# Attention scores of two heads in the two halves of the array, with three score tasks a pair

## The chip, the cores and the metric

The kernel runs on one core of one Trainium2 chip. A core has TensorE (PE), VectorE (DVE), ScalarE (ACT), GpSimd (POOL), and SyncE (SP), which here only issues DMAs. Each engine works through its own list of instructions in order, and they meet at semaphores. The metric is the device time of one execution in microseconds; the kernel before takes 745.94 us (median of 3 runs, 744.32 to 747.05).

## The reference

Two blocks on an input of 2 batches x 512 positions x 512 channels. Block 0 is attention with 32 heads of 16 channels, times a gated feed-forward, plus the input; block 1 (a small recurrent net and an octonion feed-forward) is not touched by the change beyond the names of its PSUM banks. What matters is block 0's attention:

```python
qkv = hidden_states @ qkv_w + qkv_b
q, k, v = jnp.split(qkv, 3, axis=-1)            # 32 heads of 16
q = _rope(q, cos, sin)
k = _rope(k, cos, sin)
scores = jnp.einsum('bqhd,bkhd->bhqk', q, k) * scale
scores = scores + (1.0 - causal) * MASK_VAL
probs = jax.nn.softmax(scores, axis=-1)
ctx = jnp.einsum('bhqk,bkhd->bqhd', probs, v).reshape(b, s, e)
return ctx @ out_w + out_b
```

## The kernel before

Every fp32 product is made of three products of a reduced type (`f32r`): high x high, high x low, low x high. For a projection these are three matmuls over 128 rows, here called a triple (`passes`, lines 913 to 916). For the scores the parts are stacked on the contraction rows: a head's 16 channels give 48 rows. The weights of block 0 come as units of 128x512; SP loads a unit (`raw`), ACT or POOL writes its high part, POOL its low part (`split`), PE uses it.

**Scores.** Heads are worked through in 16 pairs a batch, four heads (two pairs) being a group. `q_st` holds a group's queries, both heads of a pair one above the other on 96 rows. `kz` holds the keys with zeros: for either head there is a copy in which the other head's 48 rows are zero, so that a matmul over 96 rows gives one head's scores. Each pair has two kinds of task. Five tasks of `score` (lines 932 to 945) put queries on PSUM's partitions; DVE takes the row maxima of them (`row_maxima`, a reduce or an operation that adds the causal mask and keeps the maximum), joins them, and PE turns them (`max_turn`) so that ACT can write them as extra rows into `q_st`. Five tasks of `score_T` (947 to 954), 8 slots later, compute the transposed scores over 100 rows, with the maximum subtracted by the four extra rows; `kz` has the values -1 on these rows, set on DVE at the start (line 1537) after POOL has cleared `kz` (721). ACT takes the exponential (1294), POOL clears the part above the diagonal (752), and PE multiplies with V (1065), four heads side by side in four strips of 32 columns of the array.

**Order.** Each batch is a list of slots (`SLOTS`), and each engine's program walks it. A slot s has score task s, score_T task s - 8, perhaps a piece of probs x V, and the triples of the next projection and feed-forward units (`triples_in`), which fill PE's time. Units 0 and 1 (Q and K of the first quarter) and 2 to 5 (V) come before the slots. The rotary result of Q and K is written to DRAM by head (`write_rows`) and read back stacked (`read_rows`), which takes up to the first score. Three PSUM banks (`score_ps`) are shared by both kinds of task in turn; two banks (`turn_ps`) take all transposes. After the slots with scores come 11 slots of the feed-forward's down projection, then the output projection.

## Time and profile before

| | |
|---|---|
| runs | 744.32, 745.94, 747.05 us |
| profiled execution | 744.25 us, its span 742.1 us |
| PE, DVE busy | 653.9 us (88%), 453.2 us (61%) |
| POOL, ACT busy | 403.7 us (54%), 280.3 us (38%) |
| mean granted clock of TensorE | 0.964 |
| triples of all projections (lines 914 to 916), 240 each | 100.9, 96.7 and 96.0 us |
| scores (938, 952) and transposed maxima (928) | 29.3, 65.4 and 20.0 us |

Times are in microseconds from the span's start. Matmuls are pipelined, so one that is listed with 0.39 us may be followed by the next 0.23 us later: for PE the distance from start to start tells what one costs. The fraction after an operation in a timeline, in brackets, is the idle time of the engine just before it and who ended it. The granted clock is a share of full speed.

### The profile page before, as it was taken

How to read it: one execution, taken by the hardware profiler on the slowest of the kernel's cores; microseconds unless marked ns; L12 is line 12 of the kernel's file. 1: busy time of each engine (PE TensorE's matmuls, PEld its weight loads, DVE VectorE, ACT ScalarE, POOL GpSimd, SP SyncE). 2: the span in 40 equal slices, each digit the busy share in tenths (PEclk: the TensorE clock that was granted, in tenths of full speed). 3: DMA queues.
4: the chain of work that ended last, by engine and by line, in shares of the span. 5: the costliest groups of instructions: out<-in, count | busy, mean ns of one | idle time of the engine just before them, and what ended most of it. 6: DMA issues, size and time to landing. Idle time of an engine off the chain costs nothing. (4 is left out here: it accounts for less than half of the span.)

```text
span 742.1 us, 9827 instructions
## 1 busy us (share of the span) xinstructions
PE 653.9 (88%) x3229; PEld 468.4 (63%) x3229; DVE 453.2 (61%) x1086; ACT 280.3 (38%) x501; POOL 403.7 (54%) x593
## 2 busy tenths in 40 slices
PE   1967899999989998889999998989798979797993
PEld 1756566667756776666666765678676655555571
DVE  4977778756534493887785562459454434756347
ACT  2413445444543411344444455351222534142441
POOL 6476455545343556646554534439725778344465
PEclk9989999999999999999999999999998989999997
DMA  8287575753222226967575316534200000000003
GB/s 263 80 288 227 129 203 134 212 134 77 75 72 72 57 71 198 310 151 200 140 198 144 85 36 228 190 101 160 76 1 0 1 0 1 1 0 1 0 1 113
DMA packets 59731, 82.21 MB, mean 111 GB/s; under 512 B 18057, under 2 KB 26505, under 8 KB 59681
## 3 DMA queue, kind: packets, MB, share of 16 engines
q1 hardware_dynamic: 56016, 70.31, 33.4%
q10 hardware_dynamic: 3664, 11.28, 4.1%
q8 instruction: 26, 0.43, 0.2%
q14 instruction: 25, 0.20, 0.1%
HBM read 63.75 MB, written 26.47 MB: 122 GB/s over the span
## 5 line engine op out<-in xcount | busy, mean ns | idle before, releaser
L731 POOL TENSOR_TENSOR w_lo<-raw,w_hi 128x512 fp32r<-128x512 f32 x98 | 129.3, 1321 | 81.7 <-ACT w_hi L1251 76.8
L1294 ACT ACTIVATE probs_T<-score_ps 128x512 f32<-128x512 f32 x160 | 95.8, 599 | 156.2 <-PE score_ps L952 132.9
L1444 DVE CUSTOM_DVE_ANT_0 score_ps<-score_ps,causal 128x128 f32<-128x128 f32 (+2 forms) x256 | 103.0, 447 | 52.9 <-PE score_ps L938 28.6
L914 PE MATMUL proj_ps<-xn_hi,w_hi 128*128 128x512 f32 x240 | 100.9, 420 | 12.2 <-DVE by_sin L1520 7.5
L752 POOL TENSOR_SCALAR_AFFINE_SELECT probs_T<-probs_T 128x256 f32<-128x256 f32 (+1 forms) x160 | 56.5, 362 | 96.6 <-ACT probs_T L1294 96.6
L915 PE MATMUL proj_ps<-xn_hi,w_lo 128*128 128x512 f32 x240 | 96.7, 403 | 0.0
L916 PE MATMUL proj_ps<-xn_lo,w_hi 128*128 128x512 f32 x240 | 96.0, 400 | 0.0
L952 PE MATMUL score_ps<-q_st,kz 100*128 100x512 f32 (+3 forms) x256 | 65.4, 316 | 8.6 <-DVE row_max L1444 8.4
L952 PEld LDWEIGHTS score_ps<-q_st,kz 100*128 100x128 f32 x256 | 47.8, 188 | 26.0 <-DVE row_max L1444 15.1
L914 PEld LDWEIGHTS proj_ps<-xn_hi,w_hi 128*128 128x128 f32 x240 | 47.1, 196 | 22.7 <-issue 12.3
L916 PEld LDWEIGHTS proj_ps<-xn_lo,w_hi 128*128 128x128 f32 x240 | 46.7, 194 | 11.4
L729 POOL TENSOR_SCALAR w_hi<-raw 128x512 fp32r<-128x512 f32 x56 | 36.4, 650 | 31.2 <-PE proj_ps L916 24.3
L915 PEld LDWEIGHTS proj_ps<-xn_hi,w_lo 128*128 128x128 f32 x240 | 47.3, 197 | 8.6
L1065 PE MATMUL ctx_ps<-probs_T,V 128*32 128x128 f32 (+3 forms) x512 | 47.7, 445 | 0.0
L869 POOL TENSOR_TENSOR hsL<-hidden_T,hsH 128x256 fp32r<-128x256 f32 x44 | 34.8, 805 | 21.9 <-ACT hsH L1378 21.9
L1498 DVE SCALAR_TENSOR_TENSOR gate_silu<-gate_tanh,proj_ps 128x512 f32<-128x512 f32 x22 | 15.1, 686 | 36.9 <-ACT gate_tanh L1260 24.4
L1592 DVE TENSOR_TENSOR hsl<-hidden_T,hsh 128x512 fp32r<-128x512 f32 x22 | 16.9, 769 | 32.4 <-ACT hsh L1309 32.4
L1444 DVE DVE_READ_ACCUMULATOR2_ANT row_max<- 128x1 f32 x256 | 35.8, 140 | 0.0
L740 POOL TENSOR_TENSOR rows_lo<-turned_rows,rows_hi 128x512 fp32r<-128x512 f32 x16 | 20.7, 1295 | 25.8 <-ACT rows_hi L1229 25.8
L938 PE MATMUL score_ps<-kz,q_st 96*128 96x512 f32 x64 | 29.3, 457 | 5.8 <-DMA kz<-rows 5.8
L1251 ACT ACTIVATE w_hi<-raw 128x512 fp32r<-128x512 f32 x42 | 26.2, 624 | 17.8 <-PE turn_ps L916 6.3
L1438 DVE TENSOR_REDUCE row_max<-score_ps 128x2 f32<-128x512 f32 x32 | 22.0, 688 | 16.3 <-PE score_ps L940 15.9
(288 smaller groups left out, 1496.0 us busy)
## 6 DMA issues: line engine op xcount, KB each, us to landing
raw<-w SPq DMA_DIRECT2D x98, 256.0 KB, 2.7
rows<-rows_hi SPq DMA_DIRECT2D x32, 256.0 KB, 3.6
arranged<-tern SPq DMA_DIRECT2D x96, 85.0 KB
q_st<-rows SPq DMA_DIRECT2D x16, 384.0 KB, 4.5
kz<-rows SPq DMA_DIRECT2D x32, 192.0 KB, 4.9
...
```

The lines of the kernel that those rows point to most:

```text
L729: nc.gpsimd.tensor_scalar(w_hi[n % SPLIT][:, :], raw[n % RAW][:, :], 1.0, 0.0, ALU.mult, ALU.add).then_inc(hi_done, 1)
L731: nc.gpsimd.tensor_tensor(w_lo[n % SPLIT][:, :], raw[n % RAW][:, :], F32(w_hi[n % SPLIT][:, :]), ALU.subtract).then_inc(unit_ready, 1)
L752: nc.gpsimd.affine_select(out=blocks, in_=blocks, pattern=[[0, n], [1, P]], compare_op=ALU.is_ge, fill=0.0, base=0, channel_multiplier=-1) ...
L869: nc.gpsimd.tensor_tensor(hsL[d % HS][:, :], hidden1_T[:, f, 256 * pr:256 * pr + 256], F32(hsH[d % HS][:, :]), sub).then_inc(hs1_ready, 1)
L914: nc.tensor.matmul(acc, lh, rh, start=first, stop=False)
L915: nc.tensor.matmul(acc, ll, rh, start=False, stop=False)
L916: return nc.tensor.matmul(acc, lh, rl, start=False, stop=last)
L938: return nc.tensor.matmul(acc[:, :], q[:, 3 * P:], k[:, i, :], start=True, stop=True)
L952: m = nc.tensor.matmul(acc[:, c:c + S - kt * P], k[:, hh, kt * P:(kt + 1) * P], q[:, kt * P:], start=x == 0, stop=True, skip_group_check=x ...
L1065: m = nc.tensor.matmul(ctx_ps[32 * h:32 * h + 32, kt * P:S], V[:, kt, (4 * g + h) * 32:(4 * g + h + 1) * 32], probs_T[(gp + h // 2) % 3][: ...
L1294: nc.scalar.activation(probs_T[gp % 3][:, 512 * i:512 * i + 512], score_bank(b, ("b", s - LAG))[:, :], ACT.Exp, scale=0.25).then_inc(probs ...
L1444: m = nc.vector.tensor_tensor_reduce(out=block, in0=block, in1=causal[:, S - w:], scale=1.0, scalar=-3e38, op0=ALU.add, op1=ALU.max, accum ...
```

## The change

Each head of a pair gets contraction rows of its own: head 0 has rows 0 to 49 and head 1 rows 64 to 113, in `q_st` as in the new `k_st` that takes the place of `kz`. The first two of the 50 rows belong to the maximum (in `k_st` the value -1, written to DRAM once by SP from a constant `edges` and read back with the rows), the other 48 are the head's stacked parts. A score task is now one matmul (or two) for each head, into two PSUM banks; a pair has three tasks of each kind instead of five, `LAG` goes from 8 to 5, and a batch has 53 slots with scores instead of 88. Row tasks compute no more than the part up to the diagonal block. There are two banks for the rows and two for the transposed scores, no sharing, and one bank (`one_turn_ps`) for transposes during the scores. POOL's clearing of `kz` and DVE's six operations on it are gone, as are one reduce and one joining step a pair; ACT copies the turned maxima in two pieces. The second Q and K units move from 6 and 7 to 8 and 9, and eight triples (units 6 and 7) instead of four precede slot 0. `rope_first` now has all three operations that read the projection. The high part of a hidden tile for the down projection is made two slots ahead rather than one, and the `arranged` copies are spread over slots 9 to 51.

```diff
-B_BANKS = [[(0, 0, 0)], [(0, 1, 0), (0, 3, 384)], [(0, 2, 0), (1, 2, 256)], [(1, 0, 0)], [(1, 1, 0), (1, 3, 384)]]
-LAG = 8
-SCORE_SLOTS = 5 * PAIRS + LAG
+A_TILES = [[(3, 0)], [(2, 0), (0, 384)], [(1, 0)]]
+B_TILES = [[(0, 0)], [(1, 0), (3, 384)], [(2, 0)]]
+WIDTH = (512, 512, 256)
+TASKS = 3 * PAIRS
+LAG = 5
+SCORE_SLOTS = TASKS + LAG
...
-Q_UNIT, K_UNIT, V_UNIT = (0, 6, 12, 18), (1, 7, 13, 19), 2
+Q_UNIT, K_UNIT, V_UNIT = (0, 8, 12, 18), (1, 9, 13, 19), 2
...
-    return max(-1, (k - KC) * SCORE_SLOTS // (TRIPLES - KC))
+    return max(-1, (k - 2 * KC) * SCORE_SLOTS // (TRIPLES - 2 * KC))
...
-    return next((g for g in range(1, GROUPS) if (1 if g == 1 else max(10 * g - 10, unit_slot(K_UNIT[g // 2]) + 9)) == s), None)
+    return next((g for g in range(1, GROUPS) if (1 if g == 1 else max(6 * g - 6, unit_slot(K_UNIT[g // 2]) + 7)) == s), None)
...
-            for n in range(3):
-                nc.gpsimd.memset(F32(kz[n][:, :, :, :]), 0.0).then_inc(zeroed, 1)
...
+            def stacks(b, j, hh):
+
+                n = (GROUPS * b + j // 2) % 3
+                rows = slice(64 * hh, 64 * hh + HEAD_ROWS)
+                return q_st[n][rows, j % 2, :], k_st[n][rows, j % 2, :]
+
+            def scores(b, j, x):
+
+                for part, (qt, c) in enumerate(A_TILES[x]):
+                    for hh in range(2):
+                        q, k = stacks(b, j, hh)
+                        m = nc.tensor.matmul(score_ps[:, hh, c:c + (qt + 1) * P], q[:, qt * P:(qt + 1) * P], k[:, 0:(qt + 1) * P],
+                                             start=part == 0, stop=True, skip_group_check=part > 0)
+                m.then_inc(score_done, 1)
...
                 for s in range(SLOTS):
                     if score_in(s):
...
-                        if bank_free(b, ("a", s)):
-                            pe.wait_ge(*bank_free(b, ("a", s)))
-                        score(score_bank(b, ("a", s)), b, j, i).then_inc(score_done, 1)
+                        if s:
+                            pe.wait_ge(part_ready, TASKS * b + s)
+                        scores(b, j, x)
+                    if prob_in(s):
+                        j, x = prob_in(s)
+                        if x == 0:
+                            pe.wait_ge(*copied(b, ("max", j)))
+                        if s > LAG:
+                            pe.wait_ge(probs_ready, TASKS * b + s - LAG)
+                        scores_T(b, j, x)
...
+                for qt, c in A_TILES[x]:
+                    w = (qt + 1) * P
+                    for hh in range(2):
+                        block = score_ps[:, hh, c:c + w]
+                        m = nc.vector.tensor_tensor_reduce(out=block, in0=block, in1=causal[:, S - w:], scale=1.0, scalar=-3e38, op0=ALU.add,
+                                                           op1=ALU.max, accum_out=row_max[:, j % 2, 2 * qt + hh:2 * qt + hh + 1])
...
-            for n in range(3):
-                for hh in range(2):
-                    rows = kz[n][2 * ROWS:2 * ROWS + 4, :, hh, :]
-                    nc.vector.tensor_scalar(rows, F32(rows), extreme[2 * ROWS:2 * ROWS + 4, hh:hh + 1], None, ALU.add).then_inc(extreme_set, 1)
```

PE's list around the first piece of the first probs x V product of the first batch, before. `score_ps<-kz` is a task with queries on the partitions, `score_ps<-q_st` a transposed one, `ctx_ps` the product with V, `turn_ps` the turning of the maxima.

```order
L938 MATMUL score_ps<-kz_75,q_st_88 128x512
L914 MATMUL proj_ps<-xn_hi,w_hi_103 128x512
L915 MATMUL proj_ps<-xn_hi,w_lo_108 128x512
L916 MATMUL proj_ps<-xn_lo,w_hi_103 128x512
L952 MATMUL score_ps<-q_st_87,kz_74 128x256 x2
L1065 MATMUL ctx_ps<-probs_T_91,V 32x512 x2
L1065 MATMUL ctx_ps<-probs_T_92,V 32x512 x2
L938 MATMUL score_ps<-kz_75,q_st_88 128x512
L914 MATMUL proj_ps<-xn_hi,w_hi_103 128x512
L915 MATMUL proj_ps<-xn_hi,w_lo_108 128x512
L916 MATMUL proj_ps<-xn_lo,w_hi_103 128x512
L952 MATMUL score_ps<-q_st_87,kz_74 128x512
```

The same place in PE's list now (`score_ps<-k_st` with queries on the partitions, `scoreT_ps` transposed, `one_turn_ps` the maxima):

```order
L943 MATMUL one_turn_ps<-ident,max_cols 34x128 x4
L1081 MATMUL ctx_ps<-probs_T_91,V 32x512 x2
L1081 MATMUL ctx_ps<-probs_T_92,V 32x512 x2
L957 MATMUL score_ps<-k_st_74,q_st_88 128x384 x2
L957 MATMUL score_ps<-k_st_74,q_st_88 128x128 x2
L966 MATMUL scoreT_ps<-q_st_87,k_st_73 128x256 x2
L929 MATMUL proj_ps<-xn_hi,w_hi_105 128x512
L930 MATMUL proj_ps<-xn_hi,w_lo_110 128x512
L931 MATMUL proj_ps<-xn_lo,w_hi_105 128x512
L929 MATMUL proj_ps<-xn_hi,w_hi_105 128x512
L930 MATMUL proj_ps<-xn_hi,w_lo_110 128x512
L931 MATMUL proj_ps<-xn_lo,w_hi_105 128x512
```

Both kinds of task now stand together in a slot, each as pairs of matmuls for the two heads, and two triples follow where there were one or two.

SP's list around the load of the third group's rows, before (`raw` a weight unit, `rows<-` the rotary rows to DRAM, `q_st`, `kz` the rows back):

```order
L632 DMA raw_97<-w 128x512 [waits unit_ready]
L640 DMA rows<-rows_hi_83 16x8x512 [waits rows_hi_ready]
L640 DMA rows<-rows_hi_83 16x8x512
L642 DMA rows<-rows_lo_85 16x8x512 [waits rows_lo_ready]
L632 DMA raw_98<-w 128x512 [waits unit_ready]
L656 DMA q_st_88<-rows 96x2x512 [waits extreme_set,rows_stored]
L659 DMA kz_75<-rows 48x2x512 x2
```

And now:

```order
L652 DMA rows<-rows_hi_83 16x8x512 [waits rows_hi_ready]
L652 DMA rows<-rows_hi_83 16x8x512
L654 DMA rows<-rows_lo_85 16x8x512 [waits rows_lo_ready]
L644 DMA raw_97<-w 128x512 [waits unit_ready]
L707 DMA arranged<-tern 64x2x170 [waits tern_stored]
L707 DMA arranged<-tern 64x2x170
L644 DMA raw_98<-w 128x512 [waits unit_ready]
L667 DMA q_st_88<-rows 50x2x512 [waits rows_stored]
L667 DMA q_st_88<-rows 50x2x512
L667 DMA k_st_74<-rows 50x2x512 x2
```

The load stands one weight unit and two copies further behind the rows' writing, and is four DMAs instead of three; it is used from slot 12 on, where it was from slot 20 on.

## Rows read from the trace of the kernel before

**Rows 1.** Busy time by stretch (us, share by engine, PEclk, DMA, GB/s).
```profile
47.30:67.80 20.50, 16.93 (x64) 13.42 (x65) 16.63 (x48) 3.53 (x6) 14.40 (x16) 0.84 0.77 256
67.80:214.50 146.70, 138.38 (x802) 95.90 (x800) 97.72 (x333) 69.37 (x121) 73.59 (x126) 1.00 0.51 135
...
291.60:311.10 19.50, 16.90 (x64) 13.22 (x65) 16.54 (x48) 3.53 (x6) 14.38 (x16) 0.82 0.83 268
311.10:458.50 147.40, 139.02 (x805) 96.46 (x804) 97.56 (x333) 69.18 (x120) 74.27 (x126) 1.00 0.54 144
```

**Rows 2.** Timeline of PE from 612 and 624 us: start, us, engine, line.
```profile
614.41 0.39 PE L1127 MATMUL proj_ps<-down_w,hsL 128*128 128x512 f32 x1
614.73 1.13 PE L1190 MATMUL score_ps<-wk,w1T 64*128 64x512 f32 x4
615.79 0.50 PE L1126 MATMUL proj_ps<-down_w,hsH 128*128 128x512 f32 x1
...
625.28 1.02 PE L1158 MATMUL score_ps<-wk,centre_m 128*128 128x512 f32 x2
...
626.37 0.40 PE L1113 MATMUL ctx_ps<-xm_lo,up_w 128*128 128x512 f32 x1
```

**Rows 3.** Timeline of PE around one probs x V product.
```profile
84.87 0.40 PE L952 MATMUL score_ps<-q_st,kz 100*128 100x256 f32 x2
85.19 1.07 PE L1065 MATMUL ctx_ps<-probs_T,V 128*32 128x512 f32 x8
86.19 0.50 PE L938 MATMUL score_ps<-kz,q_st 96*128 96x512 f32 x1
86.53 0.40 PE L914 MATMUL proj_ps<-xn_hi,w_hi 128*128 128x512 f32 x1
86.77 0.40 PE L915 MATMUL proj_ps<-xn_hi,w_lo 128*128 128x512 f32 x1
```

**Rows 4.** Timeline of all engines, 4 to 10 us.
```profile
4.27 5.29 POOL L721 MEMSET kz<- 128x2048 f32 x3
...
7.95 0.36 DVE L1475 BATCH_NORM_AGGREGATE mean_var<-stat 128x2 f32<-128x6 f32 x4
```

**Rows 5.** Timeline of DVE, 20 to 36 us.
```profile
20.80 8.23 DVE L1537 TENSOR_SCALAR kz<-kz,extreme 4x1024 fp32r<-4x1024 f32 x6
29.06 0.75 DVE L1511 SCALAR_TENSOR_TENSOR by_cos<-proj_ps,qk_bias,rope_cos 128x512 f32<-128x512 f32 x1
...
34.56 0.69 DVE L1527 TENSOR_TENSOR turned_rows<-by_cos,by_sin 128x512 f32<-128x512 f32 x1
```

**Rows 6.** Timeline of PE: the first start, the down stage, the second start.
```profile
24.98 0.17 PE L997 MATMUL turn_ps<-abs_sums,V 128*128 128x3 f32 x1
...
40.24 0.79 PE L914 MATMUL proj_ps<-xn_hi,w_hi 128*128 128x512 f32 x1 [3.97 <-POOL w_lo L731]
...
47.31 0.77 PE L938 MATMUL score_ps<-kz,q_st 96*128 96x512 f32 x1 [2.44 <-DMA kz<-rows]
...
59.85 0.47 PE L914 MATMUL proj_ps<-xn_hi,w_hi 128*128 128x512 f32 x1 [3.57 <-DVE by_sin L1520]
...
214.56 0.50 PE L914 MATMUL score_ps<-w_hi,hsh 128*128 128x512 f32 x1 [1.93 <-DVE hsl L1592]
...
291.66 0.47 PE L938 MATMUL score_ps<-kz,q_st 96*128 96x512 f32 x1 [3.41 <-DMA kz<-rows]
```

**Rows 7.** Groups of lines by shape (count, busy, mean ns, idle before).
```profile
L731 POOL TENSOR_TENSOR w_lo<-raw,w_hi 128x512 fp32r<-128x512 f32 x98 | 129.3, 1321 | 81.7 <-ACT w_hi L1251 76.8
...
L1444 DVE CUSTOM_DVE_ANT_0 score_ps<-score_ps,causal 128x512 f32<-128x512 f32 x64 | 44.0, 697 | 28.8 <-PE score_ps L938 28.6
...
L729 POOL TENSOR_SCALAR w_hi<-raw 128x512 fp32r<-128x512 f32 x56 | 36.4, 650 | 31.2 <-PE proj_ps L916 24.3 <-DMA raw<-w 6.3
...
L1444 DVE CUSTOM_DVE_ANT_0 score_ps<-score_ps,causal 128x128 f32<-128x128 f32 x128 | 33.3, 322 | 17.9 <-PE score_ps L943 17.6
```

**Rows 8.** The page's DMA issues (count, KB each, median us to landing).
```profile
kz<-rows SPq DMA_DIRECT2D x32, 192.0 KB, 4.9
```

444 lines of the change are left out of this document (212 added, 232 removed).

## The prediction

> **What bounds the kernel now.** I read the table of stretches first, then TensorE's timeline, then who waits for whom. The part that changes is the attention of either batch: its start, and the score stage. In the steady score stage [rows 1] (second and fourth row) PE is busy for 138.38 of 146.70 us at full clock, DVE for 97.72, POOL 73.59, ACT 69.37. So PE sets the pace there, and what it saves in that stage is worth its full price as long as DVE, the next one, does not take over. The two first stretches [rows 1] (first and third row) are different: 20.5 and 19.5 us with a granted clock of 0.84 and 0.82, and DVE busy for 16.63 and 16.54 of them, so there PE waits. TensorE's own timeline shows the places [rows 6]: 3.97 us for a weight split of POOL at 40.24, 2.44 us for the rows that come back from DRAM at 47.31, 3.57 us for DVE's rotary work at 59.85, 3.41 us for the rows again at 291.66.
>
> The profiled execution took 744.25 us (span 742.1), the median of the runs is 745.94. I make the sum against 744.25 and add 1.7 at the end.
>
> **1. Set-up of the first batch: 6.7 us earlier.** POOL's three memsets of kz, 5.29 us, end at 9.56, while DVE has the means ready at 8.31 [rows 4]; without them the norm starts 1.25 us earlier, and all of PE's first work with it. The six small DVE operations on kz, 8.23 us, go too, and they stand ahead of the rotary work of Q and K (29.06 to 35.25) [rows 5]. K's projection ends at about 25.1 [rows 6], with the shift at 23.9, and Q's about 2.7 us before it, so Q's rotation runs 21.2 to 24.2 and K's to 27.3. From K's last addition to the first score matmul before are 47.31 - 35.25 = 12.1 us (ACT's high part, POOL's low part, write, read back); four loads in place of three add about 0.4 (one issue), which gives 39.8. PE's side is later: V's projection ended at 36.27 (40.24 less the 3.97 idle), now 35.0, and then come eight fill triples in place of four, 8 x 0.70 = 5.6 us, so 40.6. POOL must have split units 6 and 7 by then: it starts about 29.3, at some 2.6 us a unit while DVE's ternary work slows it, done at 34.5. First score at 40.6 in place of 47.3, with four triples more behind it.
>
> **2. Set-up of the second batch: 0.3 us later.** There DVE's combining of the batch before bounds the rows; they land where they did, with one issue more. The 3.41 us of waiting [rows 6] is filled with the four extra triples (2.8 us); that work is taken from the score stage, where I count it.
>
> **3. First slots.** Before, ten slots (two pairs) took 20.5 and 19.5 us. Now two pairs are six slots. One maximum over 512 columns costs 0.63 us from start to start, over 128 columns 0.25 (the means 697 and 322 overlap the next start) [rows 7]; a pair's eight are 3.6 us, joining them 0.8 (an estimate: two small operations and their waits), and two rotary units of 3.1 (29.06 to 35.25 for two [rows 5]) fall into these slots. With single score banks (both of the pair in one task), PE asks for the next task only after DVE has read the last: a slot takes at least 0.55 (matmul and its way to DVE) + 1.3 to 1.5. Slot by slot that gives 16.1 us: 4.4 and 3.4 less.
>
> **4. The rest of the score stage: 11.1 us less per batch**, from 146.7 and 147.4, in three parts.
> Two heads in two halves: a matmul of 512 columns takes 0.24 us from start to start [rows 3]. A pair has 2 x 2560 columns, ten times 0.235, or 2.35 us; side by side 1.17. That halves overlap is seen in block 1 [rows 2]: four 64-row passes of 512 columns take 1.06 us (614.73 to 615.79), while two full passes of the same type take 0.85 (625.28 to 626.37, less one matmul of 0.24). One after another the four would be 1.7.
> Against it stands what a change of the array's layout costs. Around a product of probs and V [rows 3] the matmul ahead takes 0.32 in place of 0.24, the product 1.00 in place of 0.86, the one behind it 0.34: 0.32 us for in and out. Around the 64-row passes it is 0.08 ahead and 0.21 inside [rows 2]. I take 0.33. By the order of instructions, each of three slots a pair goes into the new layout and out again: 1.0 us. In four of six slots the neighbour is a probs x V product that changed the layout anyway, which gives back about 0.1 each, 0.3 a pair with the bubbles that the two small matmuls of the old fourth task had. Net 2.35 - 1.17 - 1.0 + 0.3 = 0.48 us a pair, times 14.7 pairs: 7.0 us. The Trainium skill, "TensorEngine Tiling (Array Packing)", section Key Properties, says that a change of the tiling mode drains TensorE, while two tiles of one mode run in parallel. By that rule each of these slots pays, and the trace agrees with its 0.32 us; were the layout change free, the term would be 32 x 1.0 us larger, so 32 us more of gain.
> Triples moved ahead of the stage: three fewer here (one fewer in the first slots), 2.1 us.
> Waits: PE is idle for 8.3 of the 146.7 us [rows 1], 1.9 of them at the stage's end, so some 6.5 are waits, most of them for DVE's maxima. Now DVE's load falls (no separate reduce, no joining of two parts) but a rotary unit's 2.25 us in one piece can delay the next task, about 0.4 each for four units. I take 4.5: 2 us less. Not less than 0 and up to 15 us a batch are its bounds, since DVE works for 97.72 us of 146.7 now, and for some 92 of about 136 then.
>
> **5. A new wait, 5.4 us per batch more.** The rows of the third group are asked for in slot 10 and needed in slot 12; before, slot 11 for slot 20. In SP's order the read stands behind the load of raw unit 21, which waits for POOL's split of unit 17, which waits for the end of unit 12 in slot 9. From then: 0.65 + 1.32 us for the split [rows 7], 0.4 for the load, 1.7 for four issues, 4.9 to landing [rows 8]: 8.9 us, against two slots of 2.35 to 2.45, so 4.0 us of waiting. Behind the waiting matmul stand all of slot 12's tasks. After waits of such a size the clock was at half for some 3 us ([rows 1], first and third row, 0.84 and 0.82), which costs 1.4 us more. Bounds: 0 (the loads run ahead) to 8 (they land late behind the small-packet copies).
>
> **6. Ends.** The high part of the first hidden tile is now made two slots ahead, so the 1.93 us wait of the down stage [rows 6] keeps only the last probabilities and the last unit, about 1 us: 0.9 less, twice. In the second batch ACT waits in slot 53 for copies whose last is issued in slot 51, where it had 25 slots: 1 us, 0 to 4. Exps of 1024 columns, two small copies of the maxima in place of one, masks: ACT and POOL have half their time free, nothing. All else keeps its order.
>
> **Sum.** -6.7 + 0.3 - 4.4 - 3.4 - 2 x 11.1 + 2 x 5.4 - 1.8 + 1 = -26.4: 744.25 becomes 717.9, and with 1.7 for the median 719.5. I write 719.
>
> **Rivals.**
> Rows in time and cheap changes: SP and POOL run ahead, the third group's rows land before slot 12 (-10.8), and a layout change hides half its price behind the next weight load (-16 x 0.5 = -8). For it: the pass count inside one layout change is small and two of the three pieces are below 0.1 us. Against it: the chain of waits in item 5 has no slack. 719 - 19 = 700. Chance 0.20.
> DVE becomes the pace: one pair of score banks means that each of 48 tasks a batch is handed over with PE waiting, where three banks shared the load before. If each hand-over costs 0.25 us, 96 x 0.25 = 24 us: 743, no change. For it: the first stretches [rows 1], where DVE at 81 to 85% held PE up. Against: DVE has a third of its time free in the steady stage. It decides when DVE's slot, 0.55 + maxima + unit, passes PE's 2.85 us. Chance 0.12.
> The halves do not run side by side with this operand type: then each pair loses the 1.17 us and still pays for the layouts, 32 x 1.17 = 37.5: 756.5, slower. It decides if four 64-row fp32 passes [rows 2] say nothing on the reduced type; the trace has no row-split matmul of that type. Also this is how it comes out if the change does not do what it says. Chance 0.06.
> The forecast has the remaining 0.62, with 706 to 731 as its own range.
>
> **How the numbers follow.** What a measurement of this kernel can tell from no change is about 0.5%, 3.7 us: 742 to 750 is the same. Faster: 0.62 + 0.20 + half of 0.12, 0.88. Same 0.05. Slower 0.07, the last rival and a little of the one before. The range reaches from the first rival at 702 to 738, short of the second and third.
>
> **What would show it.** The first score task at 40 to 42 us and the two heads' matmuls starting within 0.1 us of each other; matmuls of neighbours at 0.32 to 0.34 beside a layout change; a wait of 3 to 5 us of PE for k_st or q_st once in either batch, about 30 us behind the first score; the score stage some 7 to 12 us shorter behind its first two pairs; DVE busy for under 75% of it. It is wrong if the pair's matmuls start 0.2 us apart, or if PE's waits for the maxima pass 10 us a batch.

## The result and the profile after

The changed kernel takes 736.07 us (median of 4 runs, 733.23 to 738.93), the kernel before, run beside it, 745.13. The ratio is 0.9875, with an interval of 0.9842 to 0.9908. Measured once more later (label e12 below) it was 0.9828 (0.9797 to 0.9859). So the change gains 9 to 13 us, by the ratios, where 26 were forecast; single edits are compared below with the middle of the two ratios, 0.985. Since these two ratios of one and the same kernel lie 3.5 us apart and each run's own interval reaches 2 to 3 us to either side, a difference by the ratios under 3 us says nothing by itself, and the traces have to decide. One run of e9 took 795 us at a granted clock of 0.75; it is left out of that ratio, and the median given there (713.83 us) would be 713.71 without it. The profiled execution took 734.26 us, its span is 732.5 against 742.1.

The table of stretches of the profile after, cut at the same events as [rows 1] (first score, two pairs later, first product of the down stage):

```profile
40.20:60.00 19.80, 15.57 (x59) 9.86 (x58) 15.52 (x46) 3.31 (x5) 12.53 (x13) 0.83 0.89 306
60.00:200.90 140.90, 131.69 (x827) 81.14 (x827) 93.72 (x305) 73.71 (x106) 73.16 (x112) 0.98 0.51 145
280.60:300.40 19.80, 15.00 (x58) 9.59 (x58) 14.99 (x44) 2.72 (x4) 13.17 (x14) 0.83 0.68 217
300.40:442.70 142.30, 132.16 (x826) 81.35 (x826) 94.53 (x307) 73.58 (x106) 72.33 (x111) 0.97 0.54 155
```

The first two pairs take as long as they did, again at a clock of 0.83. The rest of the score stage is 5.8 and 4.4 us shorter, with a busy PE of 132 us in place of 138, and 9 to 10 us of waiting in place of 8. TensorE's timeline has the places (start, us, what; in brackets the idle time ahead and who ended it):

```profile
40.21 0.50 PE L957 MATMUL score_ps<-k_st,q_st 50*128 50x512 f32 x2
42.84 0.77 PE L929 MATMUL proj_ps<-xn_hi,w_hi 128*128 128x512 f32 x1 [2.13 <-POOL w_lo L744]
...
54.35 0.50 PE L957 MATMUL score_ps<-k_st,q_st 50*128 50x384 f32 x4 [1.96 <-DVE row_max L1459]
...
79.72 0.80 PE L957 MATMUL score_ps<-k_st,q_st 50*128 50x512 f32 x2 [5.31 <-DMA k_st<-rows]
...
200.93 0.47 PE L929 MATMUL score_ps<-w_hi,hsh 128*128 128x512 f32 x1 [1.50 <-DVE hidden_T L1516]
...
220.20 0.65 PE L925 MATMUL one_turn_ps<-ident,ctx_sums 128*128 128x128 f32 x4 [1.78 <-ACT ctx_sums L1338]
...
280.59 0.49 PE L957 MATMUL score_ps<-k_st,q_st 50*128 50x512 f32 x2 [3.25 <-DMA k_st<-rows]
283.21 0.76 PE L929 MATMUL proj_ps<-xn_hi,w_hi 128*128 128x512 f32 x1 [2.13 <-DVE gate_silu L1512]
...
321.10 0.80 PE L957 MATMUL score_ps<-k_st,q_st 50*128 50x512 f32 x2 [5.08 <-DMA k_st<-rows]
...
442.75 0.77 PE L929 MATMUL score_ps<-w_hi,hsh 128*128 128x512 f32 x1 [1.50 <-DVE hidden_T L1516]
```

They answer to [rows 6]: the first score stands at 40.21, where 40.6 was forecast, and without a wait. The wait at slot 12 is there, 5.31 and 5.08 us (the waits for `k_st`). Three kinds of wait are not in the forecast: 2.13 us right behind the first score of either batch, 1.78 us for the sums in the down stage, and 3.25 us for the rows ahead of the second batch, though four triples now fill that gap. Where a row of 512 columns is listed with 0.77 or 0.80 us instead of 0.5 or less, the clock is at half: behind 442.75 the next ones follow at 0.43 us from start to start, behind the wait at 200.93 at 0.23.

Laid end to end on the two profiled spans (the second batch's set-up is counted from the third group of the output projection, 258.36 before and 244.68 after, its down stage to the last norm's first turn, 524.41 and 513.28):

| stretch | before | after | difference | forecast |
|---|---|---|---|---|
| up to the first score | 47.31 | 40.21 | -7.1 | -6.7 |
| batch 0: first two pairs | 20.5 | 19.8 | -0.7 | -4.4 |
| batch 0: rest of the score stage | 146.8 | 140.9 | -5.8 | -6.6 |
| batch 0: down stage | 43.8 | 43.75 | 0 | 0 |
| set-up of batch 1 | 33.3 | 35.9 | +2.6 | +0.3 |
| batch 1: first two pairs | 19.4 | 19.85 | +0.4 | -3.4 |
| batch 1: rest of the score stage | 146.8 | 142.3 | -4.4 | -6.6 |
| batch 1: down stage, output | 66.55 | 70.5 | +4.0 | +1.0 |
| from the last norm to the end | 217.7 | 219.2 | +1.5 | 0 |
| sum | | | -9.6 | -26.4 |

Inside the steady stage the slots are as forecast. One slot's tasks, and the starts of the slots six earlier and six later:

```profile
134.07 0.50 PE L957 MATMUL score_ps<-k_st,q_st 50*128 50x512 f32 x2
...
151.25 0.50 PE L957 MATMUL score_ps<-k_st,q_st 50*128 50x512 f32 x2
151.58 0.40 PE L966 MATMUL scoreT_ps<-q_st,k_st 50*128 50x384 f32 x4
151.91 0.50 PE L929 MATMUL proj_ps<-xn_hi,w_hi 128*128 128x512 f32 x1
152.25 0.40 PE L930 MATMUL proj_ps<-xn_hi,w_lo 128*128 128x512 f32 x1
...
168.42 0.50 PE L957 MATMUL score_ps<-k_st,q_st 50*128 50x512 f32 x2
```

Two matmuls of 512 columns for the two heads take 0.33 us, the four of the next task 0.33, the first full one behind them 0.34: against the 0.235 each of the prediction that is 0.3 us for the way into the layout and out. Two pairs take 17.17 us.

### The profile page after: what moved, and what is told of

Same layout as the page of the kernel before. It is cut to its first block and busy times, and to the rows that moved or that the text cites. A ratio compares the mean times of both kernels' runs of the same rounds, so it can differ in the third digit from the quotient of the medians.

```text
span 732.5 us, 9833 instructions
## 1 busy us (share of the span) xinstructions
PE 644.0 (88%) x3293; PEld 437.5 (60%) x3293; DVE 434.5 (59%) x1016; ACT 288.4 (39%) x469; POOL 392.1 (54%) x559
## 5 line engine op out<-in xcount | busy, mean ns | idle before, releaser
L1459 DVE CUSTOM_DVE_ANT_0 score_ps<-score_ps,causal 128x512 f32<-128x512 f32 (+3 forms) x256 | 120.0, 517 | 91.7 <-PE score_ps L957 91.5
L1312 ACT ACTIVATE probs_T<-scoreT_ps 128x1024 f32<-128x1024 f32 (+1 forms) x96 | 84.7, 883 | 82.8 <-PE scoreT_ps L966 81.8
L930 PE MATMUL proj_ps<-xn_hi,w_lo 128*128 128x512 f32 x224 | 90.2, 402 | 0.0
L957 PE MATMUL score_ps<-k_st,q_st 50*128 50x512 f32 (+3 forms) x256 | 45.6, 393 | 22.3 <-DMA k_st<-rows 13.6
L957 PEld LDWEIGHTS score_ps<-k_st,q_st 50*128 50x128 f32 x256 | 22.1, 188 | 66.2 <-issue 34.9
L764 POOL TENSOR_SCALAR_AFFINE_SELECT probs_T<-probs_T 128x256 f32<-128x256 f32 x128 | 50.2, 414 | 20.1 <-ACT probs_T L1312 19.9
L1237 ACT ACTIVATE q_st<-one_turn_ps 2x512 fp32r<-2x512 f32 x64 | 37.5, 585 | 26.9 <-PE one_turn_ps L943 26.4
L930 PEld LDWEIGHTS proj_ps<-xn_hi,w_lo 128*128 128x128 f32 x224 | 43.8, 196 | 5.4
L1601 DVE TENSOR_TENSOR hsl<-hidden_T,hsh 128x512 fp32r<-128x512 f32 x22 | 16.1, 734 | 43.7 <-ACT hsh L1329 43.7
L1246 ACT ACTIVATE rows_hi<-turned_rows 128x512 fp32r<-128x512 f32 x16 | 10.1, 631 | 75.1 <-DVE turned_rows L1540 75.1
L966 PE MATMUL scoreT_ps<-q_st,k_st 50*128 50x512 f32 (+3 forms) x256 | 37.9, 333 | 0.6 <-ACT probs_T L1312 0.6
L1329 ACT ACTIVATE hsh<-hidden_T 128x512 fp32r<-128x512 f32 x22 | 13.9, 630 | 49.9 <-PE score_ps L931 49.9
```

The costliest lines, as they stand in the source:

```text
L764: m = nc.gpsimd.affine_select(out=halves[:, :, c:c + P], in_=halves[:, :, c:c + P], pattern=[[0, 2], [1, P]], compare_op=ALU.is_ge, fill=0 ...
L930: nc.tensor.matmul(acc, ll, rh, start=False, stop=False)
L957: m = nc.tensor.matmul(score_ps[:, hh, c:c + (qt + 1) * P], q[:, qt * P:(qt + 1) * P], k[:, 0:(qt + 1) * P], start=part == 0, stop=True, s ...
L966: m = nc.tensor.matmul(scoreT_ps[:, hh, c:c + S - kt * P], k[:, kt * P:(kt + 1) * P], q[:, kt * P:], start=part == 0, stop=True, skip_grou ...
L1237: m = nc.scalar.activation(q_st[g % 3][64 * hh:64 * hh + 2, j % 2, :], turn_bank(n)[32 * hh:32 * hh + 2, :], ACT.Copy)
L1312: nc.scalar.activation(probs_T[gp % 4][:, c:c + 2 * w].rearrange("p (h c) -> p h c", h=2), scoreT_ps[:, :, 0:w], ACT.Exp, scale=0.25).then ...
```

## The experiments

Each has one edit on the changed kernel, unless it says otherwise; "less" and "more" are against the changed kernel at 0.985 of the kernel before.

**e1. Gate and hidden product ahead of slot 0's maxima.**

```diff
+                    if s == 0:
+                        for u in units_after(0):
+                            ffn_out(b, u)
                     if score_in(s):
                         row_maxima(b, s)
```

> The changed kernel, with one edit: VectorE works off the gate and hidden product of units 6 and 7 before the row maxima of slot 0 instead of behind them. My theory (the projection banks): TensorE's 2.13 us of waiting in slot 0 of either batch is for the bank that this product frees, not for GpSimd's low part that the profile names in the first batch. Then the wait goes in both batches, with the stretch at half clock behind it: slot 1 starts at about 43.0 instead of 45.67 and at about 283.4 instead of 286.04, and the time falls by 4 to 6 us, to about 731. Rival 1 (GpSimd's low part holds it in the first batch): only the second batch gains, 2 to 3 us, 733.5. Rival 2 (VectorE is the pace of the first two pairs): slot 1 is earlier, slot 6 starts where it did (60.0 and 300.4), time 735 to 736.

Measured: 731.43 us, ratio 0.9806 (0.9767 to 0.9845), 3 us less, which the time alone does not tell from nothing. VectorE's list in the changed kernel shows what it is about (the gate waits behind both maxima):

```profile
40.75 0.70 DVE L1459 CUSTOM_DVE_ANT_0 score_ps<-score_ps,causal 128x512 f32<-128x512 f32 x1 [4.83 <-PE score_ps L957]
...
41.36 0.73 DVE L1459 CUSTOM_DVE_ANT_0 score_ps<-score_ps,causal 128x512 f32<-128x512 f32 x1
...
42.01 0.68 DVE L1512 SCALAR_TENSOR_TENSOR gate_silu<-gate_tanh,proj_ps 128x512 f32<-128x512 f32 x1
```

It ends at 42.69, TensorE goes on at 42.84; the low part that the profile named ends at 42.77 and belongs to unit 9, not to the unit that TensorE was at. With the edit, TensorE in batch 0:

```profile
42.89 0.47 PE L929 MATMUL proj_ps<-xn_hi,w_hi 128*128 128x512 f32 x1 [1.45 <-DVE gate_silu L1512]
```

Slot 1 follows slot 0 by 3.97 and 3.58 us in place of 5.46 and 5.45, and the first two pairs take 17.6 and 18.0 us in place of 19.8 and 19.85. In batch 1 the wait is gone, in batch 0 the gate now waits for ScalarE's tanh, which stands behind its ternary pieces. Rival 1 falls, the bank it is. Rival 2 falls in batch 1, where slot 12 starts 38.2 us behind slot 0 in place of 40.5, though 1.4 and 1.7 us of waiting at slot 4 stay. In batch 0 it has something for it: the same kernel without the edit took 17.9 us for the two pairs in e12, and slot 12 starts at 79.29 for 79.72, since VectorE's maxima hold TensorE in slots 6 to 8 (0.84, 0.54 and 0.82 us) where they hardly did. The profiled execution was the slowest of the six (735.24): both its down stages began at half clock, in the changed kernel's profile only the second.

**e2. The third group's rows asked for two slots earlier.**

```diff
-... max(6 * g - 6, unit_slot(K_UNIT[g // 2]) + 7)) == s), None)
+... max(6 * g - 6, unit_slot(K_UNIT[g // 2]) + 5)) == s), None)
```

> The changed kernel, with the rows of the third group asked for in slot 8 instead of slot 10. My theory: the wait at slot 12 (5.31 and 5.08 us) is the chain of weight load, four issues and landing behind the read, so it falls by what the read is issued earlier. The rows are written at 64.73 and lie in DRAM some 5 us later, so the read goes out at about 69.8 instead of 72.5 and lands at about 76.9, where TensorE stands ready at 74.4: 2.5 us of waiting in place of 5.3, in either batch; with a shorter stretch at half clock the time falls by 5 to 7 us, to about 730. Rival (the landing is set by the traffic of the small arranged copies and weight loads, or GpSimd's splits run dry because SyncE stands at the rows): the wait stays above 4.5 us or turns into a wait for w_lo, and the time is 735 to 737.

Measured: 726.14 us, ratio 0.9749 (0.9709 to 0.979), 8 us less. SyncE's list of the changed kernel has the chain (start, us of issuing):

```profile
62.54 0.33 SPq L644 DMA_DIRECT2D raw<-w  x1
62.92 1.16 SPq L652 DMA_DIRECT2D rows<-rows_hi  x2
64.12 0.61 SPq L654 DMA_DIRECT2D rows<-rows_lo  x1
67.14 0.33 SPq L644 DMA_DIRECT2D raw<-w  x1
67.52 1.40 SPq L707 DMA_DIRECT2D arranged<-tern  x2
72.12 0.33 SPq L644 DMA_DIRECT2D raw<-w  x1
72.50 0.77 SPq L667 DMA_DIRECT2D q_st<-rows  x2
73.31 0.74 SPq L667 DMA_DIRECT2D k_st<-rows  x2
```

The last write took 3.8 us from issue to landing, so the rows lay in DRAM at 67.9, 4 us before 72.12, where GpSimd's split (it ends at 72.10) let the load ahead of them go. With the edit slot 12 waits

```profile
76.84 0.50 PE L957 MATMUL score_ps<-k_st,q_st 50*128 50x512 f32 x2 [0.88 <-DVE row_max L1459]
...
315.66 0.50 PE L957 MATMUL score_ps<-k_st,q_st 50*128 50x512 f32 x2 [2.29 <-DMA k_st<-rows]
```

0.9 and 2.3 us, and no longer at half clock. The theory holds, and in batch 0 the rows are in time (2.5 us of waiting were expected); slots 6 to 12 take 16.5 and 17.9 us instead of 19.7 and 20.7. In batch 1 four loads of X stand ahead of the rows' writing (see e9).

**e3. The sums turned one slot later.** `ctx_in` counts from slot 18 instead of 17.

> The changed kernel, with the turning of each group's sums one slot later (two slots behind the last product with V, as it was before the change, instead of one). My theory: TensorE's waits for ctx_sums at the end of the score stage (0.79, 0.80) and in the down stage (1.78, 1.78) are ScalarE's copy with nothing of TensorE's beside it, so all four go: 5.1 us, to 731. Rival (they are handed on to the waits that follow, hidden_T at the stage's end and xn_lo in the down stage): less than 1.5 us, 735.

Measured: 728.39 us, ratio 0.9769 (0.9742 to 0.9796), 6 us less. Of the four waits the two in the down stages go and the two at the stage's end stay:

```profile
203.07 0.66 PE L925 MATMUL one_turn_ps<-ident,ctx_sums 128*128 128x128 f32 x4 [0.81 <-ACT ctx_sums L1338]
204.20 0.71 PE L929 MATMUL score_ps<-w_hi,hsh 128*128 128x512 f32 x1 [0.47 <-DVE hidden_T L1516]
```

The wait for hidden_T falls from 1.50 to 0.47, since VectorE's work on the turned sums is no longer ahead of it. So half of the theory was right, and the size came out by another split. The profiled execution, the slowest of the six, is only 2.0 us shorter: in the score stages a wait of 1.2 us for the turned rows (`ctx_rows`) comes in each. The second batch's down stage is 65.9 us long in place of 70.5; some 2.6 of that (thirteen matmuls 0.2 us further apart) is a stretch at half clock that followed the longer wait in the changed kernel (row at 442.75).

**e4. The rotary work behind the next slot's maxima.**

```diff
                     for u in units_after(s - 1):
                         if u in QK_OF:
+                            rope_first(b, u)
                             rope_second(b, u)
...
-                        else:
-                            rope_first(b, u)
```

> The changed kernel, with VectorE's three rotary operations of a Q or K unit moved from the end of a slot to behind the next slot's row maxima. My theory: the waits for row_max at slot 4 (1.96 and 1.67 us) and the 0.9 to 0.5 us ones of slots 6 to 8 are these 2.2 us of VectorE ahead of the maxima of a task whose bank TensorE wants, so they fall by two thirds or more: slot 6 starts at about 58.3 and 298.7, and the time falls by 3 to 5 us, to 732. Rival (the projection bank is now freed later and the unit behind waits, or the wait moves one slot on because VectorE is full in these slots anyway): 735 to 737, with waits for by_sin in place of row_max.

Measured: 738.20 us, ratio 0.9919 (0.989 to 0.9948), 5 us more. The first wait for row_max goes, and others come:

```profile
53.25 0.47 PE L929 MATMUL proj_ps<-xn_hi,w_hi 128*128 128x512 f32 x1 [1.32 <-POOL w_lo L744]
...
59.68 0.47 PE L929 MATMUL proj_ps<-xn_hi,w_hi 128*128 128x512 f32 x1 [1.13 <-DVE by_sin L1529]
```

The rival holds: the bank comes free later, and GpSimd's split with it. My theory had the cause of the wait right and the worth of the edit wrong: two pairs of batch 0 take 17.2 us for 17.9 in e12, but slot 9 starts 26.5 us behind slot 0 for 26.4 there, and the rest of the score stage is 145 us long in either batch in place of 141 to 142.

**e5. Both heads on the same rows.**

```diff
-                rows = slice(64 * hh, 64 * hh + HEAD_ROWS)
+                rows = slice(0, HEAD_ROWS)
```

> The changed kernel, but the matmuls of both heads of a pair take their operands from rows 0 to 49, so that they can't use different halves of the array (head 1's scores are head 0's: its own are left out). My theory: the two halves work side by side, and that is worth a pair's ten passes of 512 columns at 0.235 us less half of them, 1.17 us; here they run one after another, so the time rises by 32 x 1.17 = 37 us or a little less where VectorE's maxima are waited for anyway, to 768 to 774, and the two heads' matmuls start 0.2 us apart instead of together. Rival (the halves save little, the gain of the score stage is the shorter row tasks): a rise under 12 us.

Measured: 768.97 us, ratio 1.0318 (1.0281 to 1.0356), 35 us more, or 1.09 us a pair where 1.17 were worked out; in the traces the score stages behind the first two pairs are 33.1 us longer, 1.18 for each of their 28 pairs. A slot's tasks now:

```profile
152.37 0.74 PE L957 MATMUL score_ps<-k_st,q_st 50*128 50x512 f32 x2
152.95 0.68 PE L966 MATMUL scoreT_ps<-q_st,k_st 50*128 50x384 f32 x4
```

0.58 us from the first to the second task, where it was 0.33. The halves do work side by side on the reduced type; without that the kernel is 24 us slower than the one before.

**e6. A triple between the slot's two tasks.** `fill` is called for the first triple between `scores` and `scores_T`, for the others behind it.

> The changed kernel, with the slot's first triple between its score task and its transposed task, where the two tasks stand side by side. That adds one way into the 64-row layout and one out in each of 43 slots a batch. My theory (the price read from TensorE's timeline, 0.3 us for in and out): 86 x 0.3 = 26 us more, less what VectorE's and ScalarE's waits gain from the later use, so 755 to 762. Rival (the layout change hides behind the weight load, 0.1 us): 8 us or less more, up to 745.

Measured: 766.58 us, ratio 1.0295 (1.0266 to 1.0325), 33 us more, where 755 to 762 was expected, and 0.385 us for each of the 86 added ways in and out. The rival is out, and the theory's price of 0.3 is somewhat too small:

```profile
152.30 0.50 PE L957 MATMUL score_ps<-k_st,q_st 50*128 50x512 f32 x2
152.73 0.51 PE L929 MATMUL proj_ps<-xn_hi,w_hi 128*128 128x512 f32 x1
153.07 0.40 PE L930 MATMUL proj_ps<-xn_hi,w_lo 128*128 128x512 f32 x1
```

A task alone behind a product with V takes 0.43 us, and the matmul behind it 0.34: 0.3 us over two ordinary ones. Against the changed kernel's trace the 36 slots from slot 12 on are 13.3 and 12.4 us longer, 0.36 a slot; what slots 6 to 11 lose is partly taken from the wait at slot 12 (3.99 and 3.90 us). And 2.1 of the 31.3 us between the two profiled executions lie behind the last norm, where nothing was changed, so 0.385 has scatter in it. The 0.06 between 0.30 and 0.36 is open.

**e7. The set-up work put back.**

```diff
+            for n in range(3):
+                for stack in (q_st, k_st):
+                    nc.gpsimd.memset(F32(stack[n][:, :, :]), 0.0).then_inc(zeroed, 1)
...
+                for hh in range(2):
+                    part = (q_st, k_st)[hh][n][96:100, :, :]
+                    nc.vector.tensor_scalar(part, F32(part), 1.0, None, ALU.add).then_inc(extreme_set, 1)
```

> The changed kernel, with the set-up work that the change took out put back: GpSimd clears 12 KB a partition (here the stacks of q_st and k_st) ahead of everything, and VectorE does six additions over 4 x 1024 elements ahead of the rotary work. My theory (item 1 of the prediction): the norm starts 1.25 us later and the rotary work waits for 8.2 us of VectorE, so the first score starts at about 47 instead of 40.2 and the time rises by 6.7 us, to 743. Rival (it is covered by the eight triples and V's projection, which have to end before the first score anyway): 2 us or less.

Measured: 743.84 us, ratio 0.9983 (0.996 to 1.0006), 10 us more. (The clearing is six pieces of 1024 elements, 24 KB a partition as in the kernel before, not 12.) The first score starts at 48.54:

```profile
48.54 0.50 PE L962 MATMUL score_ps<-k_st,q_st 50*128 50x512 f32 x2 [1.09 <-DMA k_st<-rows]
```

That is 8.3 us later, not 6.7, with 1.09 us of waiting for the rows, whose reading is slower than in the kernel before (e15). Item 1 stands: without it the change would be worth almost nothing.

**e8. The edits of e1, e2 and e3 together.**

> The changed kernel with the three edits that gained in the runs before: gate and hidden product ahead of slot 0's maxima, the third group's rows asked for in slot 8, the turning of the sums one slot later. If each wait is its own cost they add up. From the marks in the traces: 2.2 + 1.9 us of the first six slots, 3.2 + 2.8 at slot 12, 1.0 and 1.8 twice at the stage's end and in the down stage, and about 2.4 of half clock behind them: 17 us less than the changed kernel, 718 to 720. Rival (VectorE is the pace of the first twelve slots, so the two first edits share one gain): 724 to 727.

Measured: 716.43 us, ratio 0.9605 (0.9582 to 0.9629), 18 us less, about the sum of the three (17 by their ratios; the profiled executions differ by 17.3). The theory holds, though in batch 0 the wait in slot 0 stays at 1.99 us and the two pairs at 19.3: the edit of e1 works here in batch 1 alone, where they take 16.3.

**e9. Two more edits on e8**, `ffn_tanh(b, 6)` behind the second ternary piece, and X reloaded in slot 14.

> The three edits, and two more that touch one batch each. Batch 0: ScalarE takes the tanh of unit 6 between its ternary pieces instead of behind them, since in the run before the gate product waited for it until 42.84 and TensorE still stood 1.99 us in slot 0. Batch 1: SyncE reloads X in slot 14 instead of slot 6, where its four issues (1.76 us) stood ahead of the writing of the third group's rows. My theory: slot 0's wait in batch 0 goes and with it the half clock behind it, so the first six slots take about 16.4 us instead of 19.3; the wait at slot 12 of batch 1 falls from 3.14 to about 1.4 us. Together 4 to 6 us less than the three edits (716.4): 711. Rival (the first pairs of batch 0 are VectorE's anyway): 715.

Measured: 713.83 us, ratio 0.9556 (0.9528 to 0.9583), 3.7 less than e8 by the ratios. The wait in slot 0 of batch 0 is gone, and two pairs take 16.4 us where e8 had 19.3; slots 6 to 12 of batch 1 take 16.6 in place of 18.7. Both steps came as expected, but the first two pairs of batch 1, which neither touches, take 17.5 in place of 16.3, and the sum is short of the 4 to 6 us. 16.4 is what the forecast had given the first two pairs (16.1).

**e10. On e8, the third rotary operation a slot later**, as before the change.

> The three edits, with the third rotary operation given back to the second part, a slot later, as it was before the change. If VectorE's 2.2 us in one piece are what TensorE waits for at slot 4 (1.96 and 1.03 us) and in slots 6 to 8 (0.9, 0.5, 0.8), each of these falls by up to 0.75: 3 to 5 us less in all, 712. Rival (what the run with all three operations behind the maxima showed: the bank is freed a slot later, and a wait for by_sin takes its place): 716 or a little more.

Measured: 722.20 us, ratio 0.9684 (0.9648 to 0.9719), 6 us more than e8. The first waits shrink (0.87 at slot 4), but by_sin is waited for and the rest of the score stage is 2.1 and 2.7 us longer. So the change's one-piece `rope_first`, which the forecast had as a small loss, is a gain: 6 us by the ratios, 3.5 between the profiled executions.

**e11. On e8, the parts of a hidden tile one slot ahead** (`down_in(s + 1)`).

> The three edits, with the high and low part of a hidden tile made one slot ahead instead of two, as before the change. My theory: two slots ahead gained the start of the down stage only if ScalarE is not kept from other work; the wait for xn_lo (1.63 us, before 0.98) is ScalarE's high parts ahead of xn_hi, so it falls to 1.0, but the stage's start waits again, 1.9 us in place of 0.47. Sum +1 us a batch: 718. Rival (the two-slot lead gained nothing): 715 to 716.

Measured: 712.59 us, ratio 0.9555 (0.9529 to 0.9581), 3.7 less than e8. My theory is wrong: the stage's start gets shorter too, one wait of 0.65 us in place of 0.79 and 0.47, and that for xn_lo is 0.98 for 1.63. In both batches that is 2.5 us; the rest of the gain is not located at the edit.

**e12. The changed kernel again.**

> The changed kernel once more, without an edit, beside the same runs of the kernel before as the three others. It says what the comparisons of single edits can tell: if the ratio is again 0.984 to 0.991, read_early's 0.9749 and ctx_late's 0.9769 are gains of 7 to 9 us, more than their marks in the traces (5 to 6); if it is lower, the gains by the marks are right. In its trace the same waits should stand (2.13, 1.7 to 2.0, 5.3, 5.1, 1.5, 1.78), while the stretches at half clock may lie elsewhere. I expect 736 with the waits the same, and the part from the last norm to the end at 218 to 220 us.

Measured: 733.83 us, ratio 0.9828 (0.9797 to 0.9859). The waits are the same (2.13, 1.69, 5.65, 1.49, 1.78, 3.16, 5.07), but the first two pairs of batch 0 take 17.9 us in place of 19.8, since the stretch behind the wait of 2.13 us ran at full clock. The wait of 2.13 us, and the one at slot 12:

```profile
43.08 0.47 PE L929 MATMUL proj_ps<-xn_hi,w_hi 128*128 128x512 f32 x1 [2.13 <-DVE gate_silu L1512]
...
79.58 0.80 PE L957 MATMUL score_ps<-k_st,q_st 50*128 50x512 f32 x2 [5.65 <-DMA k_st<-rows]
```

So 1.9 us of that term is not the kernel's. They are not won either: TensorE then waits for the maxima in slots 6 to 8 (0.90, 0.48 and 0.81 us) and 0.3 us longer at slot 12, which starts at 79.58 for 79.72. My expectation also said what a ratio below 0.984 would mean: that the gains of e2 and e3 are those that their traces show, under 6 us, and not the 8 and 6 us against 0.985. From the last norm to the end it takes 219.2; over all kernels here, none of which touches that part, it is 217.7 to 221.4, so the table's +1.5 is no effect of the change that could be told.

**e13. One slot ahead alone, on the changed kernel.**

> The changed kernel with one edit: the parts of a hidden tile one slot ahead instead of two. If the lead keeps ScalarE and VectorE from the work that TensorE waits for, the waits at the stage's start (0.80 for ctx_sums, 1.50 for hidden_T) shrink together to some 1.5 us, xn_lo from 1.63 to 0.98, and the turn's 1.78 stays, since it is the turning one slot early: the time falls by 3 to 4 us, 731. Rival (the gain seen on top of the other edits needs the later turning): 734 to 736, with a wait of 1.9 us for hsl at the stage's start, as in the kernel before.

Measured: 728.38 us, ratio 0.9774 (0.9751 to 0.9797), 6 us less. The wait of 1.78 us goes as well, which I had put down to the early turning. ScalarE's list of the changed kernel shows why:

```profile
218.51 0.63 ACT L1329 ACTIVATE hsh<-hidden_T 128x512 fp32r<-128x512 f32 x1 [2.16 <-PE score_ps L931]
219.05 0.61 ACT L1268 ACTIVATE w_hi<-raw 128x512 fp32r<-128x512 f32 x1
219.57 0.58 ACT L1338 ACTIVATE ctx_sums<-ctx_ps 128x512 f32<-128x512 f32 x1
```

There are two buffers for the high part. Two slots ahead, ScalarE waits at hsh until TensorE has ended its last product of the slot, and only then comes to the sums that TensorE wants next. One slot ahead, it is through with them when TensorE gets there:

```profile
229.33 0.66 PE L980 MATMUL one_turn_ps<-ident,xn_later 128*128 128x128 f32 x4 [0.98 <-DVE xn_lo L1450]
...
442.49 0.50 PE L929 MATMUL score_ps<-w_hi,hsh 128*128 128x512 f32 x1 [2.27 <-DVE hsl L1601]
```

The wait for xn_lo is 0.98 us again, and at the stage's start one wait of 2.27 us stands in place of 0.80 and 1.50. So the lead gained nothing there, and the later turning (e3) was a second cure for the same illness: the two gave 6 us each alone and 9.7 together (e11). In the traces the lead costs 4.9 us, two waits of 1.78 and twice 0.65 at xn_lo.

**e14. All six edits.**

> All six edits: gate and hidden product first, third group's rows in slot 8, the turning one slot later, tanh of unit 6 earlier, X reloaded in slot 14, hidden parts one slot ahead. The first two to four touch the start and slot 12, the others the down stages, so they should add: 712.6 with the lead of one slot, less 2.6 for the two last edits of the start: 709 to 711. Rival (what is left is VectorE's rotary work in slots 4 to 8 and the gains overlap there): 712 to 713.

Measured: 709.30 us, ratio 0.9513 (0.9493 to 0.9534). On top of e8 they add: its 0.9605 less the 0.0049 of e9 and the 0.0050 of e11 is 0.9506.

**e15. On e14, a stack read by one load over 128 partitions.**

```diff
-                    for hh in range(2):
-                        sp.dma_start(F32(stack[n % 3][64 * hh:64 * hh + HEAD_ROWS, :, :]),
-                                     rows_d[b][t][c][h + hh:h + 4:2].rearrange("p r s -> r p s")).then_inc(stack_in[n % 3], 16)
+                    sp.dma_start(F32(stack[n % 3][:, :, :]),
+                                 rows_d[b][t][c][h:h + 4].rearrange("(p a) r s -> (a r) p s", a=2)).then_inc(stack_in[n % 3], 16)
...
```

> The six edits, and each stack read by one load over 128 partitions (64 rows a head, 14 of them padding that is written to DRAM once) instead of two over 50: two loads of 512 KB in place of four of 200 KB in all 800. My theory (a load over 50 partitions moves at half the rate): from VectorE's last rotary operation of the second batch to the first score it takes 10.5 to 11 us, as in the kernel before, instead of 13.0, so the wait for k_st at the second batch's first score falls from 3.26 to 0.5 to 1 us, those left at slots 6 and 12 go, and the time falls by 2 to 4 us, to about 706, if the padding's writes cost nothing. Rival (the traffic beside it is the cause, and 28% more bytes make it worse): the wait for k_st stays at 3 us or more, 709 to 712.

Measured: 707.49 us, ratio 0.9491 (0.9468 to 0.9515). By the ratios that is 1.6 us under e14, within what the two intervals leave open. The wait for k_st at the second batch's first score falls from 3.26 to 1.39 us, but at slot 12 of the first batch one of 1.60 comes. From the end of VectorE's last rotary operation ahead of the second batch's first score to that score it takes 11.2 us, in e14 and in the changed kernel 13.05, in the kernel before 10.5. The busy share of the 16 DMA engines (tenths) and the traffic in 40 slices, in the changed kernel from 272.5 to 280.6:

```profile
DMA  0000000341366666776746999979999999998899
GB/s 10 0 0 0 0 0 10 111 51 30 142 243 263 233 233 202 243 182 142 172 131 222 344 324 273 293 192 314 222 192 212 172 162 162 162 162 162 243 405 364
```

and in e15 from 261.5 to 267.6:

```profile
DMA  0000000099318999597799999999999999999999
GB/s 0 0 0 0 0 0 0 0 94 107 40 67 322 363 363 403 201 295 228 282 416 403 403 403 430 430 376 403 403 403 430 390 403 416 376 403 430 376 376 416
```

The changed kernel's engines stand at 0.6 to 0.7 in the first half of the read, until the weight loads behind it join in, e15's at 0.9, with 28% more bytes. The form of the loads is the cause, not the traffic beside them.

**e16 and e17. Which property of the form.** e16 is e15 with four loads over 64 partitions; e17 is e14 (50 rows, no padding) with each load split into one over 48 and one over 2 partitions.

> The kernel of the run before (padded rows), with four loads over 64 partitions in place of two over 128. Theory A (what counts is how many of the 16 DMA engines a load spreads over, and 50 partitions spread over fewer): in the trace of the changed kernel the mean busy share of the DMA engines stands at 0.6 to 0.7 during the read, which is what 10 of 16 would give. Four loads over 64 partitions should then run at 0.9 and near 400 GB/s, and from VectorE's last rotary operation of the second batch to the first score it takes 11.2 us and the two issues more, 11.6 to 11.9. The Trainium skill, 'DMA: Bandwidth & Descriptors', section Why a DMA increments its semaphore by 16 and not by 1, states the rule: the largest number up to 16 that divides the slowest dimension on both sides, so 10 for 50 partitions, 16 for 64. Theory B (the number of loads): 13 us or more, with 28% more bytes. Time 707 to 709 by A, 710 to 712 by B.

> The six edits with the rows unpadded, each load over 50 partitions split into one over 48 and one over 2: eight loads a read in place of four, the same bytes. Theory A (the spread over DMA engines): the large loads run at 0.9 of the DMA engines' time; four issues more cost about 1.4 us, so rotary to score takes 11.5 to 12.5 us in place of 13.05. Theory B (the number of loads): 14 us or more. Time 708 to 710 by A, above 711 by B.

Measured: e16 714.20 us, ratio 0.9578 (0.9547 to 0.9609); e17 710.08 us, ratio 0.9537 (0.949 to 0.9583). From rotary work to score it takes 12.7 and 12.1 us. Its parts, in us:

| loads of a read | issuing | then to the score | both | DMA share, GB/s of a part of the read |
|---|---|---|---|---|
| before: 96 and twice 48 partitions | 1.3 | 4.2 | 5.5 | 1.04, 272 |
| e14: four over 50 | 1.5 | 6.0 | 7.5 | 0.67, 221 |
| e15: two over 128 | 0.9 | 4.9 | 5.8 | 1.04, 401 |
| e16: four over 64 | 2.6 | 4.5 | 7.1 | 1.05, 268 |
| e17: four over 48, four over 2 | 2.7 | 4.3 | 7.0 | 1.03, 248 |

(The parts are 287.6 to 291.6, 263.6 to 265.4, 264.5 to 267.5, 270.4 to 275.5 and 263.0 to 268.5 us. A packet that overlaps the next counts twice, so that all 16 engines busy come out a little above 1.)

SyncE's list of e16 and TensorE's first score there:

```profile
268.44 1.27 SPq L668 DMA_DIRECT2D q_st<-rows  x2
...
269.76 1.26 SPq L668 DMA_DIRECT2D k_st<-rows  x2
```

```profile
275.57 0.49 PE L961 MATMUL score_ps<-k_st,q_st 50*128 50x512 f32 x2 [2.93 <-DMA k_st<-rows]
```

Only the loads over 50 partitions leave DMA engines idle, as theory A has it; e17, twice as many loads with the same bytes, came at 12.1 us where A said 11.5 to 12.5 and B 14 or more. e16's 12.7 lies between the two theories, and its time above both. What A missed there is the issuing: a load over 64 partitions takes 0.63 us to issue, one over 50 took 0.37, so e16 loses again most of what it gains (its first read of all takes 3.6 us to issue where e15's takes 0.9, and its first score stands at 42.81 for 40.30); in batch 0 it waits 4.5 us at slot 12. And the idle engines are not the whole price: with all of them busy, e16 and e17 move 268 and 248 GB/s and e15 401, and no run here says why. From the first issue to the score e16 and e17 are only 0.4 and 0.5 us faster than e14. Why e16's time is 5 us above what A allowed is not traced to its end. e17 can't be told from e14 by its time. e15 has the lowest median of all kernels here, 5% under the kernel before.

## Why the forecast was wrong

**Item 1, right.** First score at 40.21 for 40.6; e7 shows the set-up work as its cause.

**Item 2, wrong by 2.3 us.** "One issue more" priced the issue and not the moving: from the last issue on, loads over 50 partitions bring the data 1.1 to 1.8 us later than any other form (e15 to e17), 1.8 later than the loads before, and the issues come to 0.2 more; the other 0.5 us lie between the rotary work and the first issue. Item 5 had the same blind spot. The Trainium skill has a rule that speaks against just this step of the change, in "DMA: Bandwidth & Descriptors", section Why a DMA increments its semaphore by 16 and not by 1: a load is spread over the largest number of DMA engines up to 16 that divides the slowest dimension of both its sides, which is 10 for 50 partitions and 16 for 48, 64, 96 or 128. The busy share of 0.6 to 0.7 in the trace agrees (10 of 16 is 0.63), and so does 0.67 where sixteen engines show as 1.03 to 1.05. The forecast did not weigh it. That a full spread moves at a full rate is not shown: e16 and e17 had the spread and not the rate.

**Item 3, the first step that failed: forecast 16.1 us for two pairs, measured 19.8 and 19.85.** The maxima and the rotary work were priced as they ran. What was left out is the wait for a bank: units 6 and 7, now ahead of slot 0, each hold a projection bank until VectorE's gate and hidden product, which stand behind slot 0's maxima in its list: 2.13 us, twice (e1, e9). The rotary operations in one piece cost 1.7 to 2.0 us at slot 4, not 0.4, but pay for themselves later (e10). The rest is half clock behind the waits, in batch 0 in some runs and not in others: 19.8 us in one execution and 17.9 in the next (e12). Where the first of these was gone or at most 1.5 us (e1, e8, e9, e11 and e14 to e17) the two pairs take 16.1 to 18.2 us, and 16.4 in batch 0 of e9. VectorE has more to say in these slots than the forecast gave it: what is gained ahead of slot 6 is in part lost again to its maxima in slots 6 to 8 (e4, e12).

**Item 4, right in both disputed prices.** Side by side is worth 1.09 to 1.18 us a pair for 1.17 (e5); in and out cost 0.3 in the timeline and 0.36 to 0.385 by e6, for 0.33. The Trainium skill's rule, "TensorEngine Tiling (Array Packing)", section Key Properties, that a change of the tiling mode drains TensorE while tiles of one mode run in parallel, agrees with both.

**Item 5, right in place and size:** 5.31 and 5.08 us of waiting for 4.0, with half clock behind it. Its chain is as forecast (e2). Items 4, 5 and the first half of 6 together were to give 6.6 us a batch and gave 5.8 and 4.4.

**Item 6, the second step that failed: "all else keeps its order".** It was said of the down stages without following ScalarE's list there. The hidden part two slots ahead was booked as 0.9 us of gain twice; it costs 5 to 6 us in all (e13), because with two buffers a lead of two is a wait for TensorE. The wait of ScalarE for the copies did not appear: the loads go out at 439.97, right behind its other work.

Of the 16.8 us between the forecast's and the measured difference of the spans (26.4 and 9.6), 7.5 are item 3, 3.0 the rest of the score stages, 2.3 the read-back, 3.0 the down stage of batch 1 beyond the 1.0 forecast, and 1.5 scatter of the last part, less 0.4 of item 1. The 3.0 us of batch 1's down stage are item 6's: its two longer waits are 1.5 us more than before, the half clock behind 442.75 is 2.6, and the 1.0 forecast for the copies did not come. Batch 0's down stage, 0 in the table, is no exception: the kernel before ran it at a mean granted clock of 0.96 and was busy for 41.4 us, the changed kernel at 1.00 for 39.8, and lost the same to its two longer waits (1.78 and 1.64 for 0.91 and 0.98). That it met the forecast is luck. The rivals: the halves one after another was excluded by e5; of the first rival, cheap layout changes by e6 and rows in time by the waits at slot 12. VectorE as the pace (743) was wrong for the steady stage (93.7 of 140.9 us busy, and 1.3 us of waits for the maxima between 60 and 200 us) and had something for it in the first nine slots.
